# Dense adjacency matrices built by one-hot matmuls: float32 against bf16, with weights and sigmoids in three bf16 parts

## The chip, the cores and the metric

The kernel runs on one core of one Trainium2 chip. The metric is the device time of one execution in microseconds, shorter being better.

## The reference

A chain of four graph layers over 6250 nodes of 128 features and 200,000 edges (`src`, `dst`, sorted by `dst`), each ahead of which the features are normalised:

```python
h = relu(layernorm(x)); x = x + L0(h)   # edge score * sigmoid(sum(edge_attr_16)), segment mean
h = relu(layernorm(x)); x = x + L1(h)   # agg = segment_sum(x[src], dst)
h = relu(layernorm(x)); x = x + L2(h)   # two layers: agg = segment_sum(x[src] * w[:, None], dst)
h = relu(layernorm(x)); x = x + L3(h)   # attention over the edges, softmax by dst
```

L0, L1 and L2 need, for each pair of nodes, the number of edges between them, the sum of their edge weights and the sum of their sigmoids, so three dense matrices.

## The kernel before

The first stage builds the three matrices. Edges are cut into tiles of 128 and destinations into pairs of neighbouring nodes; a *step* is one tile of edges against one pair of destinations, and there are BSTEPS = 4704 of them. For a step, `place_hot` (128 edges x 128 places, one-hot by the low part of the source number, field F_LO) is TensorE's stationary operand, and `prod` (128 edges x 300 columns) the moving one. Its 300 columns are three segments of SEG = 100: COUNTED is a one-hot of 98 columns by block and parity (F_Q), WEIGHTED and SIGMOID are the same one-hot times the edge's weight (F_W) and sigmoid (F_SIG), and the last two columns of a segment hold F_DST. The sums accumulate in four banks of PSUM (`banks`), one per pair, in turn.

Four engines take part, tied by semaphores:

- VectorE makes `place_hot` and `prod` for BATCH = 8 steps at once (`make_steps`), in two buffers each; batch i waits until the steps of batch i - 2 are done (`step_added`).
- TensorE (`add_steps`) has per step a matmul of two zero columns that opens the next bank (line 1035, waiting on `pair_copied` for the copy of step j - 2) and the main matmul (line 1040). At every fourth step it first loads two sets of four bank numbers into registers (lines 1027 and 1030).
- ScalarE (`copy_pairs`) copies 3 x 100 columns of the previous pair's bank into `evac` at every step (line 888), behind the main matmul of step j - 1 and its own last copy; at every fourth step it loads two sets of four registers (lines 875 and 878).
- SP stores a round of 16 steps (`evac`, three transfers of 800 KB) to the matrices `adj` in memory (line 554); a round's store waits for the one ahead of it, and `evac` has two halves.

Every 128 steps (a *chunk*) a new table of the steps' fields is needed: an indirect DMA brings the rows `step_stage`, VectorE shifts them (`shift_rows`), TensorE transposes the five fields into PSUM (`turn_step_rows`, line 1015), and ScalarE copies them to `step_tab` (`take_tab`, lines 863 and 864). The loops over two chunks are unrolled. The stages behind this one read `adj` and don't change.

## Time and profile before

| | |
|---|---|
| median of 3 runs | 8950.64 us (8950.48 to 8950.79) |
| the profiled execution | 8941.34 us, span 8939.4 us |
| matrices are built | 146 to 4131 us of the span |
| TensorE, share of the span busy | 79% |
| VectorE, ScalarE, GpSimd | 42%, 30%, 20% |
| mean granted clock | 0.916 of 2.4 GHz |

A row names a line of the kernel, an engine (PE TensorE, PEld its weight loads, PEldq its sequencer, DVE VectorE, ACT ScalarE), what is written and read, and its size. Times of matmuls are modelled and overlap: the distance from start to start says more than a duration. A float32 matmul stands as two rows. In brackets stands how long the engine was idle ahead of a row, and what released it. "issue" is idle time for which no releaser is seen.

### The profile page before, as it was taken

To read this page: it belongs to the slowest core of one execution; us is meant where nothing else is said; L and a number is where in the kernel's file an instruction comes from. 1 tells how busy PE (TensorE), PEld (TensorE's weight loads), DVE (VectorE), ACT (ScalarE), POOL (GpSimd) and SP (SyncE) were. 2 spreads that over 40 slices of the span, in tenths; PEclk is the share of its full clock that TensorE was granted. 3 is DMA by queue.
4 is the path that set the end of the run, shared out by engine and by line. 5 is a ranking of instruction groups with operands and counts; after the bars stand their busy time and mean duration, and the time that the engine had idled before them with its cause. 6 is when DMAs were issued, how large, how long until landed. Compare 5 with 4: busy or idle time off the path is not lost.

```text
span 8939.4 us, 161519 instructions
## 1 busy us (share of the span) xinstructions
PE 7083.8 (79%) x43583; PEld 5299.3 (59%) x43583; DVE 3710.8 (42%) x6066; ACT 2678.1 (30%) x7276; POOL 1800.6 (20%) x1742
## 2 busy tenths in 40 slices
PE   3888888888888888888999999999954566565656
PEld 1444444444444444446999999999953444443444
DVE  5555555555555555554222111111122334333333
ACT  2444444444444444443111110000021122221222
POOL 1000000000000000000000000000037777777772
PEclk9999999999999999999999999999976777777777
DMA  6444444444444444446666666776622222222221
GB/s 190 189 182 187 185 185 186 185 187 183 189 180 186 185 187 186 180 187 250 258 258 270 276 277 277 279 279 278 276 60 54 57 57 55 57 54 57 56 57 35
DMA packets 261018, 1545.71 MB, mean 173 GB/s; under 512 B 56005, under 2 KB 88469, under 8 KB 233680
## 3 DMA queue, kind: packets, MB, share of 16 engines
q1 hardware_dynamic: 201528, 1406.81, 40.3%
q0 software_dynamic: 58704, 129.89, 6.0%
q8 instruction: 346, 5.67, 0.3%
q14 instruction: 310, 2.54, 0.1%
q10 hardware_dynamic: 130, 0.80, 0.0%
HBM read 795.79 MB, written 743.11 MB: 172 GB/s over the span
## 4 chain that ended last, share of the span: by engine, by line
PE 61%; issue 11%; ACT 10%; POOL 6%; ACTq 6%; DVE 4%; DMA 2%; SPq 0%; DVEq 0%; POOLq 0%
PE psum L1074 25%; PE psum L1040 23%; ACT field L888 8%; POOL field L778 5%; PE psum L1263 4%; PE psum L1241 4%; ACTq L878 2%; PE psum L1035 2%; ACTq L875 1%; ACTq L888 1%; ACT field L979 1%; DVE work L1767 1%; DMA field<-head_table,cmp 1%; DVE work L1771 1%; PE psum L1261 1%
## 5 line engine op out<-in xcount | busy, mean ns | idle before, releaser
L1040 PE MATMUL psum<-field 128*128 128x300 f32 x9408 | 3165.8, 468 | 30.2 <-DVE field L1475 4.7
L888 ACT COPY field<-psum x4704 | 1921.6, 408 | 2050.1 <-PE psum L1040 1040.8
L1074 PE MATMUL psum<-field 128*128 128x128 f32 x19208 | 2254.8, 277 | 23.6 <-issue 18.5
L1074 PEld LDWEIGHTS psum<-field 128*128 128x128 f32 x19208 | 2231.9, 189 | 24.0 <-issue 24.0
L1040 PEld LDWEIGHTS psum<-field 128*128 128x128 f32 x9408 | 1446.4, 194 | 612.2 <-issue 519.7
L778 POOL DMA_INDIRECT field<-head_table,cmp x1563 | 1630.5, 1043 | 476.3 <-issue 456.5
L1035 PEld LDWEIGHTS psum<-zero_b 128*128 128x128 bf16 x4704 | 462.9, 98 | 1442.9 <-issue 1246.8
L1035 PE MATMUL psum<-zero_b 128*128 128x2 bf16 x4704 | 801.4, 170 | 628.0 <-issue 405.2
L1470 DVE TENSOR_TENSOR field<-iota,field 128x784 f32<-128x784 f32 x588 | 574.0, 976 | 1636.9 <-PE psum L1040 1634.5
L1475 DVE TENSOR_TENSOR field<-field 128x784 f32<-128x784 f32 x1176 | 1090.9, 970 | 0.0
L722 POOL DMA_INDIRECT field<-tile_rows,step_t_i x37 | 40.3, 1090 | 3663.1 <-PE psum L1015 3619.2
L979 ACT COPY field<-psum x1611 | 432.0, 268 | 1022.5 <-PE psum L1263 701.4
L1263 PE MATMUL psum<-field,params 128*128 x3222 | 734.4, 348 | 1.2 <-issue 0.2
L1471 DVE TENSOR_TENSOR field<-iota,field 128x1024 f32<-128x1024 f32 x588 | 716.5, 1219 | 0.0
L1263 PEld LDWEIGHTS psum<-field,params 128*128 128x128 f32 x3222 | 538.1, 209 | 61.7 <-issue 1.8
L1819 DVE TENSOR_TENSOR params<-iota,cmp 128x1024 f32<-128x1024 f32 x202 | 247.2, 1224 | 662.7 <-PE psum L1263 662.7
L1241 PE MATMUL psum<-field,cmp 128*1 128x132 f32 x3126 | 477.6, 317 | 51.4 <-DVE field L1816 51.4
L928 ACT COPY work<-psum 128x128 f32<-128x128 f32 x196 | 52.3, 267 | 1546.5 <-PE psum L1114 1546.5
L732 POOL DMA_DIRECT2D tab_d<-field x3 | 4.6, 1518 | 2346.4 <-DVEq L1675 2333.3
L1261 PE MATMUL psum<-zero_b 128*128 128x2 bf16 x1611 | 283.4, 176 | 170.7 <-ACT field L979 169.0
L1241 PEld LDWEIGHTS psum<-field,cmp 128*1 128x1 f32 x3126 | 280.6, 95 | 215.0 <-DVE field L1816 56.0
L1207 PE MATMUL psum<-ident,field 128*64 128x128 f32 (+1 forms) x100 | 25.5, 408 | 449.5 <-DMA field<-head_table,cmp 449.5
(276 smaller groups left out, 2599.0 us busy)
## 6 DMA issues: line engine op xcount, KB each, us to landing
adj<-field SPq DMA_DIRECT2D x882, 800.0 KB, 4.9
field<-adj SPq DMA_DIRECT2D x196, 3200.0 KB, 10.0
field<-head_table,cmp POOLq DMA_INDIRECT x1563
field<-in_edge_attr SPq DMA_DIRECT2D x4, 3072.0 KB, 25.0
head_table<-field SPq DMA_DIRECT2D x7, 476.0 KB, 3.3
right_edges<-zeros SPq DMA_DIRECT2D x1, 3328.0 KB, 19.8
place_rows<-right_edges SPq DMA_DIRECT2D x25, 128.0 KB, 2.8
out<-X SPq DMA_DIRECT2D x6, 448.0 KB
```

Source lines behind the costliest of these rows:

```text
L778: pool.indirect_dma_start(out=rows3[:, (i * WIN + t) * ROW3:(i * WIN + t + 1) * ROW3], out_offset=None, in_=head_table, in_offset=bass.Ind ...
L888: act.copy(evac[half][:, :, bass.ds(place[j % 4], SEG)], banks[:, bass.ds(bank[j % 4], NSEG * SEG)].rearrange("p (w c) -> p w c", w=NSEG)) ...
L979: act.copy(AGGX[:, bass.ds(at[j % 4], AGG_W)], banks[:, bass.ds(bank[j % 4], AGG_W)]).then_inc(block_copied, 1)
L1035: pe.matmul(banks[:, bass.ds(after[j % 4], 2)], zero_b[:, :], zero_b[:, 0:2], start=True, stop=True, skip_group_check=True)
L1040: pe.matmul(banks[:, bass.ds(cur[j % 4], NSEG * SEG)], place_hot[buf][:, j % BATCH, :], prod[buf][:, j % BATCH, :], start=False, stop=True ...
L1074: mm = pe.matmul(ps_y[slot][:, 0:D], source[:, hi, :], adj_in[slot][:, :, 2 * hi:2 * hi + 2], start=(hi == 0), stop=(hi == NB - 1))
L1241: mm = pe.matmul(ps_seam[0:1, 0:AGG_W], win_tab[:, i, T_CARRY, e:e + 1], rows[:, i * WIN + e, :, 0:DH3 + 1], start=(e == 0), stop=(e == ti ...
L1261: pe.matmul(banks[:, bass.ds(after[j % 4], 2)], zero_b[:, :], zero_b[:, 0:2], start=True, stop=True, skip_group_check=True)
L1263: pe.matmul(banks[:, bass.ds(cur[j % 4], AGG_W)], hot3[:, t // SUB % HOTS, j % SUB, :], rows3[:, bass.ds(row[j % 4], ROW3)].rearrange("p ( ...
L1470: dve.tensor_tensor(first, counting(HI2), per_step(F_Q, HI2), ALU.is_equal).then_inc(group_hot, 1)
L1471: dve.tensor_tensor(hot, counting(P), per_step(F_LO, P), ALU.is_equal)
L1475: ins = dve.tensor_tensor(pr[:, :, seg * SEG:seg * SEG + HI2], first, per_step(field, HI2), ALU.mult)
```

## The change

The one-hots are made in bf16, where 0 and 1 are exact. A weight or sigmoid is split into three bf16 parts (the value rounded, the rest rounded, the rest of the rest), each times the one-hot gives a segment of its own, and TensorE adds them up in PSUM: `prod` has 1 + 2 x 3 = 7 segments, and the one matmul of 300 columns becomes one of 300 (counts and first parts) and two of 200 (second and third parts) into the same bank, with the same stationary operand. In `prod` and `place_hot` the eight steps of a batch are innermost: a step's columns lie 8 elements of 2 bytes apart. The small comparison against `iota` becomes one against `iota_b`, a bf16 table in the same order, made once. `split_parts` makes the parts, once per chunk.

```diff
--- before.py
+++ after.py
@@ -42,7 +42,10 @@
 BANKS = 4
 SLOTS = PAIRS + 2 * ROUND
 FIELDS = 5
-F_LO, F_Q, F_W, F_SIG, F_DST = range(FIELDS)
+F_LO, F_Q, F_DST, F_W, F_SIG = range(FIELDS)
+PLAIN = 3
+PARTS = 3
+TAB_FIELDS = PLAIN + 2 * PARTS
 COUNTED, WEIGHTED, SIGMOID = range(NSEG)
 KINDS = 4
 R_CUR, R_NEXT, R_PREV, R_PLACE = range(KINDS)
@@ -210,10 +213,12 @@
 
         piece = carve(arena)
         evac = [piece(NSEG * ROUND * SEG).rearrange("p (w c) -> p w c", w=NSEG) for _ in range(2)]
-        prod = [piece(BATCH * NSEG * SEG).rearrange("p (s c) -> p s c", s=BATCH) for _ in range(2)]
-        place_hot = [piece(BATCH * P).rearrange("p (s c) -> p s c", s=BATCH) for _ in range(2)]
+        prod = [piece(BATCH * (1 + 2 * PARTS) * SEG // 2).bitcast(BF16).rearrange("p (c s) -> p c s", s=BATCH) for _ in range(2)]
+        place_hot = [piece(BATCH * P // 2).bitcast(BF16).rearrange("p (c s) -> p c s", s=BATCH) for _ in range(2)]
         step_stage = [piece(FIELDS * P).rearrange("p (k e) -> p k e", k=FIELDS) for _ in range(2)]
-        step_tab = [piece(FIELDS * P).rearrange("p (k s) -> p k s", k=FIELDS) for _ in range(2)]
+        step_tab = [piece(TAB_FIELDS * P // 2).bitcast(BF16).rearrange("p (k s) -> p k s", k=TAB_FIELDS) for _ in range(2)]
+        iota_b = piece(P * BATCH // 2).bitcast(BF16).rearrange("p (c s) -> p c s", s=BATCH)
+        step_rest = piece(2 * P).rearrange("p (k s) -> p k s", k=2)
 
         piece = carve(arena)
         adj_in = [piece(BPAIRS * SEG).rearrange("p (g c) -> p g c", c=SEG) for _ in range(CRING)]
@@ -258,7 +263,7 @@
         psum = ctx.enter_context(nc.psum_tensor("psum", [P, 8 * BANK], F32))
         ps = [psum[:, i * 2 * BANK:(i + 1) * 2 * BANK] for i in range(4)]
         banks = psum[:, 0:BANKS * BANK]
-        ps_tab = [psum[:, 4 * BANK:5 * BANK], psum[:, 5 * BANK:5 * BANK + P]]
+        ps_tab = [psum[:, 4 * BANK:4 * BANK + PLAIN * P], psum[:, 5 * BANK:5 * BANK + 2 * P]]
         ps_y = [psum[:, i * BANK:i * BANK + 2 * D] for i in range(CRING)]
         ps_t = psum[:, 3 * BANK:3 * BANK + D]
         ps_kv = psum[:, 4 * BANK:4 * BANK + 2 * D]
...
@@ -860,8 +867,8 @@
             def take_tab(c, slot):
 
                 act.wait_ge(step_rows_turned, c + 1)
-                act.copy(step_tab[slot][:, 0:4, :], ps_tab[0].rearrange("p (k s) -> p k s", k=4))
-                act.copy(step_tab[slot][:, 4, :], ps_tab[1]).then_inc(step_tab_ready, 1)
+                act.copy(step_tab[slot][:, PLAIN:PLAIN + 2, :], ps_tab[1].rearrange("p (k s) -> p k s", k=2))
+                act.copy(step_tab[slot][:, 0:PLAIN, :], ps_tab[0].rearrange("p (k s) -> p k s", k=PLAIN)).then_inc(step_tab_ready, 1)
 
             def copy_pairs(k, n):
 
@@ -1011,8 +1018,10 @@
                 pe.wait_ge(step_rows_shifted, c + 1)
                 if not (isinstance(c, int) and c == 0):
                     pe.wait_ge(step_tab_ready, c)
+                    pe.wait_ge(step_parts_taken, c)
                 for i in range(FIELDS):
-                    mm = pe.transpose(ps_tab[i // 4][:, i % 4 * P:(i % 4 + 1) * P], step_stage[slot][:, i, :], ident[:, :])
+                    at = i % PLAIN * P
+                    mm = pe.transpose(ps_tab[i // PLAIN][:, at:at + P], step_stage[slot][:, i, :], ident[:, :])
                 mm.then_inc(step_rows_turned, 1)
 
             def add_steps(k, n):
@@ -1037,8 +1046,14 @@
                     if j % BATCH == 0:
                         pe.wait_ge(batch_ready, k * (PER_LOOP * CHUNK // BATCH) + (j // BATCH + 1))
                     buf = j // BATCH % 2
-                    pe.matmul(banks[:, bass.ds(cur[j % 4], NSEG * SEG)], place_hot[buf][:, j % BATCH, :], prod[buf][:, j % BATCH, :],
-                              start=False, stop=True, skip_group_check=True).then_inc(step_added, 1)
+                    hot, pr = place_hot[buf][:, :, j % BATCH], prod[buf][:, :, j % BATCH]
+                    pe.matmul(banks[:, bass.ds(cur[j % 4], NSEG * SEG)], hot, pr[:, 0:NSEG * SEG],
+                              start=False, stop=True, skip_group_check=True)
+                    for part in range(1, PARTS):
+                        col0 = (1 + 2 * part) * SEG
+                        mm = pe.matmul(banks[:, SEG:][:, bass.ds(cur[j % 4], 2 * SEG)], hot, pr[:, col0:col0 + 2 * SEG],
+                                       start=False, stop=True, skip_group_check=True)
+                    mm.then_inc(step_added, 1)
                     if at == CHUNK // 2 and not isinstance(k, int):
                         turn_step_rows(k * PER_LOOP + slot + 1, (slot + 1) % 2)
 
@@ -1437,8 +1452,8 @@
             dve.wait_ge(tile_rows_stored, 32)
             for i in range(2):
                 c.then(dve.memset(evac[i], 0.0))
-                c.then(dve.memset(prod[i][:, :, HI2:SEG], 0.0))
-                c.then(dve.memset(prod[i][:, :, SEG + HI2:2 * SEG], 0.0))
+                c.then(dve.memset(prod[i], 0.0))
+            c.then(dve.tensor_copy(iota_b, iota[:, :].rearrange("p (c s) -> p c s", s=1).to_broadcast([P, P, BATCH])))
             dve.sem_inc(banks_cleared, 2)
 
             def shift_rows(c_, slot, u=0):
@@ -1449,6 +1464,20 @@
                     ins = dve.tensor_scalar(t, t, col(step_off[:, i, :], c_), None, ALU.add)
                 ins.then_inc(step_rows_shifted, 1)
 
+            def split_parts(chunk, slot):
+
+                tab = step_tab[slot]
+                whole = ps_tab[1].rearrange("p (k s) -> p k s", k=2)
+                dve.wait_ge(step_tab_ready, chunk + 1)
+                dve.tensor_tensor(step_rest, whole, tab[:, PLAIN:PLAIN + 2, :], ALU.subtract).then_inc(step_parts_taken, 1)
+                dve.wait_ge(step_parts_taken, chunk + 1)
+                dve.tensor_copy(tab[:, PLAIN + 2:PLAIN + 4, :], step_rest).then_inc(part_ready, 1)
+                dve.wait_ge(part_ready, chunk * 3 + 1)
+                dve.tensor_tensor(step_rest, step_rest, tab[:, PLAIN + 2:PLAIN + 4, :], ALU.subtract).then_inc(part_ready, 1)
+                dve.wait_ge(part_ready, chunk * 3 + 2)
+                dve.tensor_copy(tab[:, PLAIN + 4:PLAIN + 6, :], step_rest).then_inc(part_ready, 1)
+                dve.wait_ge(part_ready, chunk * 3 + 3)
+
             def make_steps(k, n):
 
 
@@ -1456,24 +1485,22 @@
                     slot, at = i * BATCH // CHUNK, i * BATCH % CHUNK
                     hot, pr, tab = place_hot[i % 2], prod[i % 2], step_tab[slot]
                     if at == 0:
-                        dve.wait_ge(step_tab_ready, k * PER_LOOP + (slot + 1))
+                        split_parts(k * PER_LOOP + slot, slot)
 
                     dve.wait_ge(step_added, k * (PER_LOOP * CHUNK) + (i * BATCH - BATCH + ADDED0))
 
                     def per_step(field, m):
-                        return tab[:, field, at:at + BATCH].rearrange("p (s a) -> p s a", a=1).to_broadcast([P, BATCH, m])
-
-                    def counting(m):
-                        return iota[:, 0:m].rearrange("p (a m) -> p a m", a=1).to_broadcast([P, BATCH, m])
-
-                    first = pr[:, :, 0:HI2]
-                    dve.tensor_tensor(first, counting(HI2), per_step(F_Q, HI2), ALU.is_equal).then_inc(group_hot, 1)
-                    dve.tensor_tensor(hot, counting(P), per_step(F_LO, P), ALU.is_equal)
-                    dve.tensor_tensor(pr[:, :, 2 * SEG + HI2:3 * SEG], counting(2), per_step(F_DST, 2), ALU.is_equal)
+                        return tab[:, field, at:at + BATCH].rearrange("p (a s) -> p a s", a=1).to_broadcast([P, m, BATCH])
+
+                    first = pr[:, 0:HI2, :]
+                    dve.tensor_tensor(first, iota_b[:, 0:HI2, :], per_step(F_Q, HI2), ALU.is_equal).then_inc(group_hot, 1)
+                    dve.tensor_tensor(hot, iota_b, per_step(F_LO, P), ALU.is_equal)
+                    dve.tensor_tensor(pr[:, SIGMOID * SEG + HI2:(SIGMOID + 1) * SEG, :], iota_b[:, 0:2, :], per_step(F_DST, 2), ALU.is_equal)
                     dve.wait_ge(group_hot, k * (PER_LOOP * CHUNK // BATCH) + (i + 1))
-                    for seg, field in ((WEIGHTED, F_W), (SIGMOID, F_SIG)):
-                        ins = dve.tensor_tensor(pr[:, :, seg * SEG:seg * SEG + HI2], first, per_step(field, HI2), ALU.mult)
-                    ins.then_inc(batch_ready, 1)
+                    parts = pr[:, SEG:, :].rearrange("p (k c) s -> p k c s", c=SEG)[:, :, 0:HI2, :]
+                    dve.tensor_tensor(parts, first.rearrange("p (a c) s -> p a c s", a=1).to_broadcast([P, 2 * PARTS, HI2, BATCH]),
+                                      tab[:, PLAIN:, at:at + BATCH].rearrange("p k (a s) -> p k a s", a=1)
+                                      .to_broadcast([P, 2 * PARTS, HI2, BATCH]), ALU.mult).then_inc(batch_ready, 1)
                     if at == CHUNK // 4 and not isinstance(k, int):
                         shift_rows(k * PER_LOOP + slot + 1, (slot + 1) % 2, k + slot)
```

Line numbers of the order rows below are each kernel's own. A register operation or a wait stands as ISA or REGISTER_ALU.

TensorE, before, one step inside a group of four (line 1035 zero matmul, 1040 main matmul):

```order
L1034 REGISTER_ALU
L1035 ISA
L1035 MATMUL psum<-zero_b 128x2
L1040 ISA
L1040 MATMUL psum<-field 128x300
```

and in the changed kernel (1044 the zero matmul, 1050 the matmul of 300 columns, 1054 those of the second and third parts):

```order
L1043 REGISTER_ALU
L1044 ISA
L1044 MATMUL psum<-zero_b 128x2
L1050 ISA
L1050 MATMUL psum<-field 128x300
L1054 ISA
L1054 MATMUL psum<-field 128x200 x2
```

One register operation and two matmuls came in behind the main one; what comes ahead of it stays.

VectorE, before, the wait and one batch of eight steps (1470 the one-hot of 98, 1471 `place_hot`, 1472 the F_DST columns, 1475 the two products):

```order
L1461 ISA
L1470 TENSOR_TENSOR field<-iota,field 128x8x98
L1471 TENSOR_TENSOR field<-iota,field 128x1024
L1472 TENSOR_TENSOR field<-iota,field 128x8x2
L1473 ISA
L1475 TENSOR_TENSOR field<-field 128x8x98 x2
```

and in the changed kernel, with the split at the start of a chunk ahead of the batch (1472 to 1479 `split_parts`, 1496 to 1498 the comparisons, 1501 the product):

```order
L1472 TENSOR_TENSOR field<-psum,field 128x256
L1474 CAST field<-field 128x256
L1475 ISA
L1476 TENSOR_TENSOR field<-field 128x256
L1477 REGISTER_ALU
L1478 CAST field<-field 128x256
L1479 REGISTER_ALU
L1490 ISA
L1496 TENSOR_TENSOR field<-field 128x784
L1497 TENSOR_TENSOR field<-field 128x1024
L1498 TENSOR_TENSOR field<-field 128x16
L1499 ISA
L1501 TENSOR_TENSOR field<-field 128x6x784
```

The two products of 784 elements became one of 6 x 784, and four operations of 256 elements came in once per chunk.

## Rows read from the trace of the kernel before

**Rows 1.** The page: the span.

```profile
span 8939.4 us, 161519 instructions
```

**Rows 2.** Busy us (x instructions), clock, DMA share, GB/s, adjacency stage.

```profile
146.25:4131.10 3984.85, 3331.55 (x14290) 1929.12 (x14288) 2348.82 (x3013) 1939.90 (x4775) 37.86 (x35) 0.98 0.46 185
```

**Rows 3.** Groups by line, 300 to 4000 us: busy us, mean ns, idle before.

```profile
L1040 PE MATMUL psum<-field 128*128 128x300 f32 x8704 | 2931.6, 468 | 24.2 <-issue 3.4
L888 ACT COPY field<-psum x4352 | 1777.8, 408 | 1904.5 <-PE psum L1040 965.1 <-issue 548.3 <-ACT field L888 389.2
L1475 DVE TENSOR_TENSOR field<-field 128x784 f32<-128x784 f32 x1088 | 1009.4, 970 | 0.0
L1471 DVE TENSOR_TENSOR field<-iota,field 128x1024 f32<-128x1024 f32 x544 | 662.9, 1219 | 0.0
L1470 DVE TENSOR_TENSOR field<-iota,field 128x784 f32<-128x784 f32 x544 | 531.1, 976 | 1528.4 <-PE psum L1040 1528.4
```

**Rows 4.** Timeline, a group with short register loads: start, us, what, [idle].

```profile
2192.88 0.41 ACT L888 COPY field<-psum  x1 [0.19 <-PE psum L1040]
2193.81 0.41 ACT L888 COPY field<-psum  x1 [0.52 <-PE psum L1040]
2194.13 0.17 PE L1035 MATMUL psum<-zero_b 128*128 128x2 bf16 x1
2194.43 0.41 ACT L888 COPY field<-psum  x1 [0.22 <-PE psum L1040]
2194.74 0.17 PE L1035 MATMUL psum<-zero_b 128*128 128x2 bf16 x1
```

**Rows 5.** Timeline, a group with long register loads.

```profile
2003.49 0.41 ACT L888 COPY field<-psum  x1 [0.19 <-ACT field L888]
2005.11 0.10 PEld L1035 LDWEIGHTS psum<-zero_b 128*128 128x128 bf16 x1 [1.81 <-issue]
2005.23 0.30 PEld L1040 LDWEIGHTS psum<-field 128*128 128x128 f32 x2
2005.68 0.41 ACT L888 COPY field<-psum  x1 [1.79 <-issue]
```

**Rows 6.** The four register loads, by line: duration ns min/median/max.

```profile
L1027 PEldq TENSOR_LOAD <-bank_rows x1176: 327/335/1360, 138.8 to 4127.9; - x196
L1030 PEldq TENSOR_LOAD <-bank_rows x1176: 325/329/996, 139.4 to 4128.3; - x196
L875 ACTq TENSOR_LOAD <-bank_rows x1176: 303/311/1017, 140.2 to 4128.4; - x196
L878 ACTq TENSOR_LOAD <-bank_rows x1176: 302/307/1159, 140.7 to 4128.7; - x196
```

**Rows 7.** TensorE in a row elsewhere: chain of waits, timeline, groups by line.

```profile
5000.62 11.27 PE psum L1074 x98
...
303.67 0.71 PE L1015 MATMUL psum<-ident,field 128*128 128x128 f32 x5
...
138.48 1.33 PE L1015 MATMUL psum<-ident,field 128*128 128x128 f32 x5 [80.16 <-DVE field L1449]
...
6773.23 1.04 PE L1207 MATMUL psum<-ident,field 128*64 128x128 f32 x4 [138.45 <-DMA field<-head_table,cmp]
...
L1015 PE MATMUL psum<-ident,field 128*128 128x128 f32 x185 | 26.9, 277 | 80.2 <-DVE field L1449 80.2
...
L1207 PE MATMUL psum<-ident,field 128*64 128x128 f32 x96 | 24.9, 414 | 449.5 <-DMA field<-head_table,cmp 449.5
```

**Rows 8.** Groups by line, VectorE's scans, 6700 to 8900 us.

```profile
L1767 DVE TENSOR_TENSOR_SCAN work<-params,work 64x512 f32<-64x512 f32 x48 | 59.7, 1243 | 1.6
...
L1747 DVE TENSOR_TENSOR_SCAN work<-field,right,place_rows 64x128 f32<-64x128 f32 x92 | 36.9, 457 | 3.3 <-DVE field L1744 1.2
...
L1784 DVE TENSOR_TENSOR_SCAN work<-work 4x64 f32<-4x64 f32 x24 | 6.7, 278 | 0.8
```

**Rows 9.** Timeline, VectorE before the stage.

```profile
128.04 4.06 DVE L1439 MEMSET field<- 128x4800 f32 x1 [7.70 <-issue]
```

More of the change, by code:

```diff
@@ L306, in build @@
         step_tab_ready = sem("step_tab_ready")
+        step_parts_taken = sem("step_parts_taken")
+        part_ready = sem("part_ready")
         banks_cleared = sem("banks_cleared")
```

## The prediction

> **What bounds the kernel now.** I read the page first, then one row of busy times for the stretch in which the adjacency matrices are built, then the groups by line, and then the timeline inside that stretch. The changed code works only in this stretch, from the first main matmul to the last: 3984.85 us of the 8939.4 us span, for 4704 steps [rows 1 to 3]. That is 0.847 us a step, or 3.39 us for the group of four steps whose bank numbers are loaded together (1176 groups). The rest of the span does not change.
>
> TensorE looks like the bound: 3331.55 us busy of 3984.85 [rows 2]. The timeline says something else. Inside a group, steps follow each other at 0.61 to 0.62 us on TensorE (zero matmul at 2194.13 and at 2194.74) and the copies that empty the banks at 0.62 on ScalarE (2193.81, 2194.43) [rows 4]. Where ScalarE alone sets the pace, the copy costs 0.41 and the wait for its own predecessor 0.19, together 0.60: the 0.19 stands in brackets behind copies [rows 5]. So both engines stand at 0.60 to 0.62. Between groups both load two sets of four registers. Short loads take 0.33 us each on TensorE's sequencer and 0.31 on ScalarE's, long ones up to 1.0 us or more [rows 6]. With short loads the copy before and the copy after them start 0.93 apart (2192.88, 2193.81) [rows 4], with long ones 2.19 (2003.49, 2005.68) [rows 5]. So a group costs ScalarE 3 x 0.60 + 0.93 = 2.73 us at best and 3 x 0.60 + 2.19 = 3.99 at worst. With the long kind for the share of time in which stores run, 0.46 [rows 2], the mean is 0.54 x 2.73 + 0.46 x 3.99 = 3.31, against 3.39 measured. **ScalarE's copies and the register loads nearly explain the stage without TensorE's arithmetic.** What a faster matmul can win is small.
>
> **The change, part by part.**
>
> *TensorE's array.* Removed: one float32 matmul of 300 columns, done as two passes (8704 rows for 4352 steps [rows 3]), which with its loads and the zero matmul makes the 0.62 us. Added: three bf16 matmuls of 300 + 200 + 200 = 700 columns, whose columns lie 16 bytes apart, and three loads of 128 weights, 16 bytes apart too. No row shows a lone 2-byte column at such a step, so I bound it. Below: five contiguous float32 transposes in 0.71 us, of which one lasts 0.27, give 0.11 us per 128 columns in float32, 0.86 ns each [rows 7]; two bytes instead of four would be 0.43 ns, or 0.30 us for 700. Above, from three rows. Matmuls over the adjacency blocks read pairs of 8 bytes 400 bytes apart: 98 of them in 11.27 us, 0.115 us for 64 pairs, 1.80 ns a pair [rows 7]. So a fresh place costs at most 1.80 ns there. VectorE's scan over 128 elements 16 bytes apart takes 457 ns, while 64 contiguous take 278 [rows 8]; with 2.15 ns an element (1243 ns for 512) the contiguous 128 would be 416, so here the element costs about 2.5 ns, 1.75 us for 700. The third row speaks for cheap reads: at 1.2 GHz (0.21 us a transpose where the five at 2.4 GHz take 0.11) four transposes whose 64 weights lie 544 bytes apart start their last matmul 1.04 - 0.41 = 0.63 after the first (one lasts 0.41), exactly 3 x 0.21; five with 128 contiguous weights 1.33 - 0.41 = 0.92, which is 4 x 0.21 and 0.07 more for the first load [rows 7]. So 64 scattered weights took at most half as long as 128 contiguous ones, whose load is some 0.1 us (0.08 of it sticks out of the present step): about 0.85 ns each, where 1.80 ns would have stuck out. I take 0.85: 700 columns 0.60, first weight load 0.08 (the present step has 0.62 - 2 x 0.25 - 0.03 for it), zero matmul 0.03: **0.70 to 0.72 us a step**, about 2.85 a group. At 0.43 ns it is 0.41.
>
> *TensorE's sequencer.* A register operation, a weight load and a matmul take it 0.12 us (weight loads at 2005.11 and 2005.23, nothing else to wait for [rows 5]). The present step has two such and an addition (some 0.09), 0.33. The change adds another such and one load and matmul without a register operation (some 0.08, both estimates from the 0.12): 0.53 us. All register loads wait behind this. With short loads a group is 4 x 0.53 + 2 x 0.33 + 0.12 between them = 2.90, with long ones 4 x 0.53 + 1.9 + 0.12 = 4.14. Today the same sum is 2.1 and 3.3, and that slack is what the copies hide. It is gone.
>
> *VectorE.* Removed per batch of eight steps: 976 + 1219 + 2 x 970 ns [rows 3], with a small one of 0.17. Added: the same two comparisons in bf16 and one product of 6 x 784 = 4704 elements. At today's 1.04 ns an element and 0.16 fixed (784 in 0.97) the product is 5.06 and the batch 7.4 us. At half the bytes and half the time the batch is 0.57 + 0.69 + 0.17 + 2.61 = 4.0, what it is today, against 6.8 us for eight steps. I take 4.0, hidden behind TensorE; if that cover goes, the rival below prices it. The Trainium skill, "VectorE: DVE Perf Modes", section "The perf-mode tier table", has two-operand operations at twice the rate in bf16 and at one for float32; the float32 half agrees with [rows 3], the other no run here shows. The four split operations per 128 steps are some 2 us in a row before the batch at a chunk's start. VectorE is 2.8 us ahead there, so about 0.
>
> *ScalarE.* Two copies out of PSUM per 128 steps as now. Nothing changes: 0.
>
> *Stores.* Each 16 steps send three blocks of 800 KB as now; nothing moves but their share of time.
>
> *Start.* The two clears of the product buffer become 2 x 2800 words instead of some small ones; 4800 words took 4.06 us [rows 9], so 2.4 each, and a conversion about 1: +6 us, all engines wait for it.
>
> *The sum.* With short loads three limits stand together, 2.73 (copies), 2.85 (array) and 2.90 (sequencer), where now there is one. Engines that wait on each other two steps apart lose something each time: I put the group at 3.0. With long loads 4.14 + 0.05 = 4.2. The stores keep their amount, 0.46 x 3.39 = 1.56 us a group, of the new 3.55, so 0.44: 0.56 x 3.0 + 0.44 x 4.2 = 3.53. Now: 3.39, of which 0.08 are loop ends and the like that stay, already above the 3.31. On the same footing (3.31 to 3.53, and the five transposes a chunk no longer hidden, below 0.02 a group) I take +0.19 x 1176 = +223 us. **8941.34 + 223 + 6 = 9170 us** for the profiled execution (its time is the span and 2 us); the median of the plain runs is 9 us above it, which I leave out. Its own range is 8990 to 9350.
>
> **The rivals.**
>
> *1. A lone column 16 bytes on is dear (27%).* At 1.80 ns: 1.26 for columns, 0.23 for the weight load, 0.03: 1.52 us a step, 4704 x 1.52 = 7150. The register loads then hide behind the array, loop ends add 0.1 ms: 8941 - 3985 + 7270 = 12,230 us. At 2.5 ns: 1.75 + 0.32 + 0.03 = 2.1 a step, 14,900 us. It decides from about 0.9 ns a column on. For it: the pairs cost 0.115 us where contiguous float32 columns cost 0.108, and VectorE's scan. Against: the strided weights. The Trainium skill, "SBUF — State Buffer", has under "Specifications (TRN2)" 16-byte lines that need two hits each for full bandwidth, and every column here would be a first and only hit; it gives no price.
>
> *2. Faster: the copies alone set the pace (18%).* If TensorE's sequencer issues the two added pairs in well under 0.1 us each and the array needs 0.41 us a step, only ScalarE's 3.31 a group is left, without the losses of today: up to 0.08 x 1176 = 94 us less; if long loads also grow rarer because VectorE and TensorE read less, 0.2 a group, 235 us. Time 8700 to 8900. For it: slack of 0.2 us a step on the array. Against: the sequencer's 0.53. It decides where a step's issue is below 0.48 us.
>
> *3. VectorE keeps one element a cycle (5%).* 7.4 us and 0.2 of waits per batch, 588 batches: 4470 us in place of 3985, 9430 us. It decides when a batch is over 7 us.
>
> **How the numbers follow.** The likeliest case has 45%, rival 1 27%, rival 2 18%, rival 3 5%, no change 5%. The time is 9170. The range is 8750 to 12,400: it leaves out the dearer half of rival 1 and the far end of rival 2. A measurement of this kernel tells 0.2% (18 us) from no change. Faster 0.19, same 0.06, slower 0.75.
>
> **What would show it.** In the new profile: the first main matmul of a step to the next step's at 0.70 in a group (right), 0.41 (free reads) or 1.5 and more (rival 1). Register loads of 0.33 and 0.9 as now. ScalarE's idle time released by TensorE, not by itself. The product of VectorE at 2.6 us (5.1 for rival 3). A granted clock of 0.9 or less in this stretch where it is 0.98 [rows 2], that is more time at 1.2 instead of 2.4 GHz, since the array idles more behind the sequencer; at 0.85 ns a column it costs little. I am wrong if a strided column costs anything but 0.4 to 0.9 ns, or if the sequencer's work overlaps what I put in a row.

## The result, and the profile after

The changed kernel takes 11,069.33 us (median of 4 runs, 11,064.25 to 11,077.3) against 8950.56 for the kernel before: 1.2369 times as long, 95% interval 1.2347 to 1.239. The page's span, to hold against [rows 1]:

```profile
span 11075.5 us, 175316 instructions
```

The stage's window (busy us of PE, PEld, DVE, ACT and POOL with their instructions, granted clock, DMA share, GB/s), to hold against [rows 2]:

```profile
154.60:6263.70 6109.10, 6045.24 (x18993) 2304.27 (x18992) 2277.81 (x2570) 1955.17 (x4775) 68.31 (x35) 1.00 0.30 121
```

The stage took 3984.85 us and takes 6109.10: 2124 of the span's 2136 us. TensorE is busy for 99% of it where it was for 84%. The groups by line, 300 to 6000 us, answer to [rows 3]:

```profile
L1054 PE MATMUL psum<-field 128*128 128x200 bf16 x8770 | 3918.5, 536 | 0.0
L1050 PE MATMUL psum<-field 128*128 128x300 bf16 x4384 | 3046.0, 695 | 0.9
L895 ACT COPY field<-psum x4384 | 1800.6, 411 | 3877.0 <-PE psum L1054 3444.4 <-issue 388.7 <-ACT field L895 42.6
L1501 DVE TENSOR_TENSOR field<-field 128x4704 bf16<-128x4704 bf16 x549 | 1427.8, 2601 | 0.0
...
L1497 DVE TENSOR_TENSOR field<-field 128x1024 bf16<-128x1024 bf16 x548 | 374.7, 684 | 0.0
L1496 DVE TENSOR_TENSOR field<-field 128x784 bf16<-128x784 bf16 x548 | 310.8, 567 | 3573.2 <-PE psum L1054 3573.2
```

VectorE now waits for TensorE alone, and ScalarE mostly (3444 of its 3877 us of idle time). A matmul's mean duration (0.695 us) is not what it costs, since matmuls overlap; the starts in the timeline are (start, us, what), to hold against [rows 4]:

```profile
2192.39 0.19 PE L1044 MATMUL psum<-zero_b 128*128 128x2 bf16 x1
2192.44 0.69 PE L1050 MATMUL psum<-field 128*128 128x300 bf16 x1
2192.95 0.89 PE L1054 MATMUL psum<-field 128*128 128x200 bf16 x2
2193.67 0.19 PE L1044 MATMUL psum<-zero_b 128*128 128x2 bf16 x1
```

A step is 1.28 us from zero matmul to zero matmul: 0.05, then 0.51 for 300 columns, then 0.72 for twice 200. Over all steps the medians of the distances between the trace's starts are 48 ns (zero matmul), 515 (300 columns), 360 and 354 (200 columns each). That is 1.72 to 1.80 ns a column. VectorE's work beside it makes no difference: the median step is 1.276 us both for the 1104 steps in which VectorE is busy throughout and for the 2385 in which it does nothing. There is no pause where register loads stand: the step that follows them is 1.276 us like the others. The loads themselves (duration ns min/median/max) are as in [rows 6]:

```profile
L1036 PEldq TENSOR_LOAD <-bank_rows x1176: 327/332/967, 146.3 to 6256.3; - x196
L1039 PEldq TENSOR_LOAD <-bank_rows x1176: 325/328/1159, 146.9 to 6256.7; - x196
```

4704 x 1.276 = 6002 us. Of the other 107, some 66 are pauses at loop ends and some 38 are the five transposes, which add 1.04 us to one step in each chunk.

### The profile page after: what moved, and what is told of

Read it like the earlier page. It is cut to its first block, busy times and chain, and to the rows that moved or that the text cites. A ratio compares the mean times of both kernels' runs of the same rounds, so it can differ in the third digit from the quotient of the medians.

```text
span 11075.5 us, 175316 instructions
## 1 busy us (share of the span) xinstructions
PE 9807.5 (89%) x48287; PEld 5681.2 (51%) x48287; DVE 3644.7 (33%) x5625; ACT 2694.8 (24%) x7276; POOL 1839.8 (17%) x1742
## 4 chain that ended last, share of the span: by engine, by line
PE 83%; POOL 6%; issue 4%; DVE 3%; DMA 1%; ACT 1%; ACTq 0%; SPq 0%; DVEq 0%; POOLq 0%
PE psum L1054 30%; PE psum L1050 24%; PE psum L1089 20%; POOL field L785 5%; PE psum L1256 3%; PE psum L1278 3%; ACT field L986 1%; DVE work L1794 0%; DVE work L1798 0%; DMA field<-head_table,cmp 0%; PE psum L1276 0%; PE psum L1024 0%; DMA field<-in_edge_attr 0%; POOL right_edges L764 0%; DMA field<-adj 0%
## 5 line engine op out<-in xcount | busy, mean ns | idle before, releaser
L1054 PE MATMUL psum<-field 128*128 128x200 bf16 x9408 | 4203.6, 536 | 0.0
L1050 PE MATMUL psum<-field 128*128 128x300 bf16 x4704 | 3268.3, 695 | 6.9 <-DVE field L1501 6.1
L1054 PEld LDWEIGHTS psum<-field 128*128 128x128 bf16 x9408 | 1445.8, 154 | 1656.8 <-issue 1656.8
L1089 PEld LDWEIGHTS psum<-field 128*128 128x128 f32 x19208 | 2233.5, 189 | 18.1 <-issue 18.1
L1496 DVE TENSOR_TENSOR field<-field 128x784 bf16<-128x784 bf16 x588 | 333.5, 567 | 3818.6 <-PE psum L1054 3818.4
L1501 DVE TENSOR_TENSOR field<-field 128x4704 bf16<-128x4704 bf16 x588 | 1529.2, 2601 | 0.0
L1050 PEld LDWEIGHTS psum<-field 128*128 128x128 bf16 x4704 | 684.2, 145 | 1067.8 <-issue 1064.1
L1044 PEld LDWEIGHTS psum<-zero_b 128*128 128x128 bf16 x4704 | 595.3, 127 | 1074.0 <-issue 1074.0
L729 POOL DMA_INDIRECT field<-tile_rows,step_t_i x37 | 70.1, 1895 | 5575.7 <-PE psum L1024 5530.8
L1044 PE MATMUL psum<-zero_b 128*128 128x2 bf16 x4704 | 876.2, 186 | 63.2 <-issue 63.2
L1276 PE MATMUL psum<-zero_b 128*128 128x2 bf16 x1611 | 283.0, 176 | 174.0 <-ACT field L986 171.8
L1497 DVE TENSOR_TENSOR field<-field 128x1024 bf16<-128x1024 bf16 x588 | 402.0, 684 | 0.0
```

Of the source, the lines that this page charges most:

```text
L1044: pe.matmul(banks[:, bass.ds(after[j % 4], 2)], zero_b[:, :], zero_b[:, 0:2], start=True, stop=True, skip_group_check=True)
L1050: pe.matmul(banks[:, bass.ds(cur[j % 4], NSEG * SEG)], hot, pr[:, 0:NSEG * SEG], start=False, stop=True, skip_group_check=True)
L1054: mm = pe.matmul(banks[:, SEG:][:, bass.ds(cur[j % 4], 2 * SEG)], hot, pr[:, col0:col0 + 2 * SEG], start=False, stop=True, skip_group_chec ...
L1089: mm = pe.matmul(ps_y[slot][:, 0:D], source[:, hi, :], adj_in[slot][:, :, 2 * hi:2 * hi + 2], start=(hi == 0), stop=(hi == NB - 1))
L1496: dve.tensor_tensor(first, iota_b[:, 0:HI2, :], per_step(F_Q, HI2), ALU.is_equal).then_inc(group_hot, 1)
L1497: dve.tensor_tensor(hot, iota_b, per_step(F_LO, P), ALU.is_equal)
```

## The experiments

### The spacing of the columns, and who pays for it

Three kernels keep the change's arithmetic, its matmuls and the number of its weight loads, and alter only how many steps lie innermost: 4 (8 bytes from column to column), 2 (4 bytes), 1 (2 bytes, side by side; the product is then six instructions). VectorE's product is cut into as many operations as there are groups of steps, or, for 1, into one per part and kind. The weights' spacing changes with the columns'; a fourth kernel, e2_weights_dense, tells the two apart. The edit, here for 2 (`...` stands for parts left out):

```
+INNER = 2
-prod = [... .rearrange("p (c s) -> p c s", s=BATCH) ...]
+prod = [... .rearrange("p (g c s) -> p g c s", g=BATCH // INNER, s=INNER) ...]
-hot, pr = place_hot[buf][:, :, j % BATCH], prod[buf][:, :, j % BATCH]
+at_g, at_s = j % BATCH // INNER, j % INNER
+hot, pr = place_hot[buf][:, at_g, :, at_s], prod[buf][:, at_g, :, at_s]
```

**s4_inner.** 

> The changed kernel with four steps innermost instead of eight: a step's columns and weights lie 8 bytes apart, so two of them share 16 bytes; VectorE's product is two operations of 2352 elements. 
Measured: 9011.85 us, 1.0063 of before (1.0046 to 1.008). Steps in a row come to 0.653 to 0.657 us, as theory 'line' said, and the total to 38 us below its range; rival 'instructions' is out. Two stretches of its timeline on TensorE:

```profile
2190.22 0.18 PE L1045 MATMUL psum<-zero_b 128*128 128x2 bf16 x1
2190.27 0.43 PE L1052 MATMUL psum<-field 128*128 128x300 bf16 x1
2190.52 0.54 PE L1056 MATMUL psum<-field 128*128 128x200 bf16 x2
2190.87 0.19 PE L1045 MATMUL psum<-zero_b 128*128 128x2 bf16 x1
...
2196.88 0.43 PE L1052 MATMUL psum<-field 128*128 128x300 bf16 x1
2197.13 0.54 PE L1056 MATMUL psum<-field 128*128 128x200 bf16 x2
2197.49 0.19 PE L1045 MATMUL psum<-zero_b 128*128 128x2 bf16 x1
```

The windows around them (the third number from the end is the granted clock: 0.50 is 1.2 GHz, 1.00 is 2.4):

```profile
2189.40:2191.00 1.60, 1.57 (x10) 1.11 (x11) 1.60 (x4) 0.82 (x2) 0.00 (x0) 0.50 0.00 0
2196.00:2198.00 2.00, 2.00 (x16) 1.44 (x15) 2.00 (x4) 0.84 (x3) 0.71 (x1) 1.00 0.87 355
```

300 columns take 0.25 us at either clock (the median is 249 ns over the 2950 steps at 1.2 GHz and also over the 1580 at 2.4), 0.83 ns each, half of what they take at 16 bytes. The 200 columns take 181 ns, again at either clock. So in this kernel the clock doesn't set the price of a column.

**s2_inner.** 

> Two steps innermost: columns 4 bytes apart, four in 16 bytes; VectorE's product in four operations of 1176 elements, 3.1 us a batch. Theory 'line': full rate, 0.42 ns a column, 0.13, 0.09 and 0.09 us, about 0.4 us of array a step; the pace is then set by TensorE's sequencer (0.53 us a step and its register loads) or by ScalarE's copies (0.60), total 8850 to 9100. If the forecast's sum for the sequencer is right it is within 1% of 8950; if copies alone bind, 8700 to 8850. Rival 'instructions': 1.28 a step, 11,050.

Measured: 8943.09 us, 0.9989 (0.9979 to 0.9998), inside the 8850 to 9100 of theory 'line'. Its timeline on TensorE:

```profile
2189.89 0.31 PE L1052 MATMUL psum<-field 128*128 128x300 bf16 x1
2190.03 0.34 PE L1056 MATMUL psum<-field 128*128 128x200 bf16 x2
2192.22 0.18 PE L1045 MATMUL psum<-zero_b 128*128 128x2 bf16 x1 [1.85 <-issue]
...
2192.97 0.41 PE L1052 MATMUL psum<-field 128*128 128x300 bf16 x1
2193.18 0.53 PE L1056 MATMUL psum<-field 128*128 128x200 bf16 x2
2193.51 0.21 PE L1045 MATMUL psum<-zero_b 128*128 128x2 bf16 x1
```

The windows of these two stretches and of the whole stage:

```profile
2189.00:2190.00 1.00, 0.69 (x5) 0.32 (x5) 1.00 (x2) 0.81 (x3) 0.00 (x0) 1.00 1.02 416
2192.90:2194.40 1.50, 1.50 (x13) 1.11 (x11) 0.00 (x0) 0.83 (x3) 0.00 (x0) 0.50 1.00 410
156.40:4131.00 3974.60, 2950.72 (x18995) 1947.57 (x18992) 2402.19 (x4331) 1945.05 (x4774) 45.46 (x35) 0.69 0.47 186
```

VectorE's product, from the groups by line:

```profile
L1512 DVE TENSOR_TENSOR field<-field 128x1176 bf16<-128x1176 bf16 x2184 | 1534.4, 767 | 0.0
```

Now 300 columns take 0.14 us at 2.4 GHz and 0.21 at 1.2. So at 2.4 GHz the array does a step in less than the old 0.617 us, and it idles, and the clock of the stage goes from 0.98 [rows 2] to 0.69: some three fifths of the steps run at 1.2 GHz, where a step is 0.61 us again.

The lower clock is not what takes the gain. ScalarE's copies cost 0.60 us a step whatever the array does (0.41 and the 0.19 that the prediction read in [rows 5]). f_s2_16 below, the kernel with the fewest register loads, shows it at full clock (granted 0.99 from 2186 to 2192 us); its copies start 0.60 apart and 3796 of its 4703 distances lie between 595 and 605 ns:

```profile
2188.27 0.41 ACT L896 COPY field<-psum  x1 [0.19 <-ACT field L896]
2188.87 0.41 ACT L896 COPY field<-psum  x1 [0.19 <-PE psum L1056]
2189.47 0.41 ACT L896 COPY field<-psum  x1 [0.19 <-ACT field L896]
```

In s2_inner, too, half of the copies start within 0.601 us of the one ahead, and what the distances have above 0.60 sums to 1.16 ms, against 1.17 in the kernel before. TensorE's register loads sum to 1.28 ms, against 1.29. So the copies and the pauses stayed, and they are the stage: 4703 x 0.60 + 1.16 = 3.98 ms. A row of steps at 1.2 GHz is 0.01 us a step longer than the copies allow; what the lower clock costs behind each pause, where a faster array could catch up, no run separates.

**s1_inner.** 

> Columns of a step side by side (step outermost), every instruction of TensorE as in the changed kernel; VectorE now reads one value again and again along the innermost direction, product in six operations of 784. Theory 'line': TensorE's matmuls 0.13, 0.09 and 0.09 us apart inside a burst, no faster than with two innermost; VectorE at one element a cycle needs 0.97 + 1.22 + 0.17 + 6 x 0.97 = 8.2 us a batch and binds, total 9700 to 9900; if it keeps two a cycle there, as with two innermost. Rival 'instructions': 1.28 a step, 11,050.

Measured: 9429.16 us, 1.0531 (1.051 to 1.0552): VectorE binds, as theory 'line' said, but the time is 270 us below its range. TensorE's intervals are those of s2_inner (135 ns for 300 columns at 2.4 GHz, 207 at 1.2). The loss is VectorE's. The window of the stage:

```profile
159.80:4617.00 4457.20, 3124.04 (x18995) 2132.99 (x18992) 4428.82 (x5505) 1943.21 (x4775) 1234.08 (x34) 0.60 0.41 166
```

The product, from the groups by line. With its factor repeated side by side it costs 1.07 ns an element again (0.993 us less some 0.15 fixed, for 784):

```profile
L1508 DVE TENSOR_TENSOR field<-field 128x784 bf16<-128x784 bf16 x2926 | 2642.7, 993 | 0.0
```

VectorE is busy for 4429 of 4457 us. A batch takes it 7.5 us (4429 over 588 batches) and not the 8.2 that was expected, since its operations overlap by some 0.09 us each: six products keep it busy for 5.4 us, not for 6 x 0.993. This is rival 3 of the prediction, in a kernel that meets its condition (a batch over 7 us).

**e2_weights_dense.** The changed kernel, whose weights are read side by side:

```
-hot, pr = place_hot[buf][:, :, j % BATCH], prod[buf][:, :, j % BATCH]
+hot = place_hot[buf].rearrange("p c s -> p (c s)")[:, j % BATCH * P:(j % BATCH + 1) * P]
+pr = prod[buf][:, :, j % BATCH]
```

> The changed kernel, but TensorE reads the 128 weights of a step side by side from the same buffer (other values, so the sums are not the reference's); the moving columns stay 16 bytes apart. Theory 'line' on the moving operand: the 0.045 us ahead of the first matmul may fall to 0.03, a step stays at 1.25 to 1.28, total 11,000 to 11,070. Rival 'weights' (four loads with scattered reads hold up the array): a step falls to 0.8 or less, total below 9500.

Measured: 11,015.59 us, 1.2303 (1.2278 to 1.2328), in the range of theory 'line'; rival 'weights' is out. Its timeline on TensorE shows 0.51, 0.71 and 0.05, nearly those of the changed kernel:

```profile
2190.01 0.69 PE L1051 MATMUL psum<-field 128*128 128x300 bf16 x1
2190.52 0.89 PE L1055 MATMUL psum<-field 128*128 128x200 bf16 x2
2191.23 0.19 PE L1044 MATMUL psum<-zero_b 128*128 128x2 bf16 x1
```

A step is 1.263 us in place of 1.276. The spacing of the weights, three loads of 128, is worth 13 ns of a step; that of the columns 0.62 us from 16 to 8 bytes alone.

### Register loads, once the array is fast

The prediction had put the register loads between groups beside the copies as what bounds the kernel before. Four kernels read 8 or 16 numbers at a time:

```
-if j % 4 == 0:
+if j % 8 == 0:
-    ... bank_rows[0:1, slot, R_CUR, at:at + 4] ...
+    ... bank_rows[0:1, slot, R_CUR, at:at + 8] ...
```

**f_before8** (the kernel before). 

> The kernel before, with eight bank numbers per register load in place of four, so the two loads on TensorE and on ScalarE come every eighth step. Theory 'copies and loads set the pace': half of what a group costs above four copies goes, about 0.4 us of the 3.28 per four steps, 1176 x 0.4 = 470 us, total 8450 to 8550. Rival 'TensorE's float32 matmul sets the pace' (3332 of 3985 us busy): at most the 0.1 to 0.2 us in which the array really idles, total above 8800.

**f_s2_8** (s2_inner). 

> Two steps innermost and eight bank numbers per load. Theory 'copies and loads': as the kernel before with eight, and a little better since the array (0.34 us a step at 2.4 GHz, 0.61 at 1.2) no longer stands beside the copies (0.60): 8350 to 8500. Rival 'the array at 1.2 GHz binds' (it idles more, so its clock falls): no better than the kernel before with eight, 8450 to 8600.

**f_s2_16** (s2_inner, 16 numbers). 

> Two steps innermost and sixteen bank numbers per load. A round of sixteen steps is then 16 x 0.60 + 0.4 to 1.6 us, about 10.6 in place of 13.1: total 8150 to 8350; it stops falling if the stores bind (three of 800 KB take 7 to 8.5 us and each round's wait for the last's), then 8350 or more. Rival 'array at 1.2 GHz': 16 x 0.61 and no gain over eight numbers beyond 50 us.

**f_after8** (the changed kernel). 

> The changed kernel (eight innermost) with eight bank numbers per load. Theory 'its array binds at 1.28 us a step and hides the loads': 11,040 to 11,075, no change. If the loads still cost something behind the array, some 200 us less.

| | expected, us | measured, us | of before |
|---|---|---|---|
| f_before8 | 8450 to 8550; rival above 8800 | 9192.03 | 1.0271 (1.0253 to 1.029) |
| f_s2_8 | 8350 to 8500; rival 8450 to 8600 | 8851.08 | 0.9891 (0.9873 to 0.9909) |
| f_s2_16 | 8150 to 8350, or more | **8813.15**, the fastest kernel of all | 0.9845 (0.9828 to 0.9863) |
| f_after8 | 11,040 to 11,075 | 11,087.28 | 1.2387 (1.236 to 1.2414) |

Theory 'copies and loads' had the price of the loads wrong: what a group costs above its copies isn't halved, and on the kernel before the edit loses. f_before8 is above 8800, but not for the reason that its rival gave, since none of that rival's terms makes it slower. f_after8 is within 18 us of the changed kernel, whose array hides the loads. TensorE's loads in f_before8 (ns min/median/max):

```profile
L1027 PEldq TENSOR_LOAD <-bank_rows x588: 587/690/2433, 137.4 to 4363.6; - x196
L1030 PEldq TENSOR_LOAD <-bank_rows x588: 585/590/1999, 138.3 to 4365.4; - x196
```

A short load of 4 numbers takes 327 ns, one of 8 takes 587, one of 16 some 1100: 65 ns a number and 67 fixed. The long ones grow in the same way, from 0.93 us to 1.83, and they are long while stores run: of the 1176 first loads of the kernel before (line 1027) 585 run while a store's transfers are in flight, and 97% of these are long; of the other 591 one is. Fewer loads save only the fixed part: TensorE's loads sum to 1.11 ms in f_before8, 1.29 before. Why the kernel before even loses shows in f_before8's timeline on TensorE:

```profile
2005.88 0.75 PE L1040 MATMUL psum<-field 128*128 128x300 f32 x2
2008.43 0.17 PE L1035 MATMUL psum<-zero_b 128*128 128x2 bf16 x1 [1.80 <-issue]
2008.64 1.36 PE L1040 MATMUL psum<-field 128*128 128x300 f32 x2
2009.80 0.21 PE L1035 MATMUL psum<-zero_b 128*128 128x2 bf16 x1
```

The windows ahead of the pause and behind it:

```profile
2004.00:2005.80 1.80, 1.80 (x10) 1.20 (x9) 0.83 (x1) 1.18 (x4) 0.00 (x0) 1.00 1.04 427
2008.70:2011.00 2.30, 2.30 (x5) 1.29 (x6) 2.30 (x6) 0.68 (x2) 0.00 (x0) 0.50 0.03 8
```

Counted from the start of a step's second pass to the next zero matmul, this pause is 2.21 us; in groups with a long load it is 2.57 on average (1.49 in the kernel before). The steps behind this one run at 1.2 GHz, where a float32 step takes 1.2 us instead of 0.62. It isn't so behind each pause (the next, with 1.86 us of idle time, is followed by steps at 2.4 GHz: granted clock 1.00 from 2023.1 to 2026 us), but behind 32% of those with a long load, against 5% in the kernel before. Counted over the stage, 543 first passes take over 0.5 us (0.64 in place of 0.336) against 124 before; with the second pass of each that is 326 us lost in place of 75. The difference, 251 us, is about the 237 us that f_before8 is slower. It is an account and not an experiment, since no run holds the clock. A bf16 step at 4 bytes loses little at 1.2 GHz, which fits the small gain that f_s2_8 keeps.

**Loads apart.** The second load of each group is moved half a group on, on both engines (TensorE's edit is shown):

```
 if j % 4 == 0:
     _, cur = ... bank_rows[0:1, slot, R_CUR, at:at + 4] ...
-    _, after = ... bank_rows[0:1, slot, R_NEXT, at:at + 4] ...
+if at == 0 or at % 4 == 2:
+    end = min(2 if at == 0 else at + 4, CHUNK)
+    after0 = j
+    _, after = ... bank_rows[0:1, slot, R_NEXT, at:end] ...
```

**g_before_apart.** 

> The kernel before, with the two register loads of each group of 4 steps two steps apart instead of back to back (on TensorE: the bank numbers of the steps at step 0 of a group, those of the banks to clear at step 2; the same for the copies' two loads on ScalarE). Nothing else changes; one more load in each 128 steps. In the kernel before, the largest pause of TensorE in a group of 4 is 432 ns on average where its two loads are short (659 ns together), and 1488 ns where at least one is long (1567 ns together). Theory 'pause': the instructions that stand ready in TensorE's queue cover about 230 ns of each pause, once; apart, they cover it twice, so a group gains about 230 ns: 1176 x 0.23 = 0.27 ms, about 8680 us. Rival 'sum': what the loads cost is their sum, wherever they stand: 8930 to 8970 us.

**g_before8_apart.** 

> The kernel before with 8 numbers per register load, and the two loads of a group of 8 steps four steps apart. With 8 per load back to back the kernel took 9192 us; its largest pause in a group with a long load was 2.57 us on average, and the rest of such a group took 5.87 us against 5.04 us in a group with short loads, for the same 8 steps, at a granted clock of 0.92 instead of 0.97 in the stage. Theory 'pause and clock': apart, a pause is one load (0.59 us short, 1.8 us long) less 230 ns, the clock falls less often, and the kernel comes back to 8550 to 8750 us. Rival 'sum': about 9190 us, and the clock stays at 0.92.

**g_s2_apart.** 

> The form with two steps innermost (8943 us), with the two register loads of a group of 4 steps two steps apart. Theory 'pause': as in the kernel before, about 230 ns a group: 8650 to 8750 us. Here the clock is mostly at its lower level and the queue issues four weight loads and four matmuls a step, so the queue itself needs 0.451 us a step and has less time to run ahead; rival 'queue': no gain, 8920 to 8960 us.

**g_s2_16_apart.** 

> The fastest form so far (two steps innermost, 16 numbers per load, 8813 us), with the two loads of a group of 16 steps eight steps apart. A load of 16 takes 1.10 us short and about 1.9 us long. Theory 'pause': each of the two loads is covered by 230 ns instead of both together: 294 groups x 0.23 = 0.07 ms, 8740 to 8790 us, and less of the clock's fall. Rival 'sum': 8800 to 8820 us.

In this batch the kernel before itself took 9670.95 us, so only ratios to it count; the expectations, in us, are divided by 8950 here:

| | expected | measured, of before |
|---|---|---|
| g_before_apart | 0.970; rival 0.998 to 1.002 | 1.1009 (1.0975 to 1.1042) |
| g_before8_apart | 0.955 to 0.978; rival 1.027 | 0.9921 (0.989 to 0.9952) |
| g_s2_apart | 0.966 to 0.978; rival 0.997 to 1.001 | 1.0885 (1.0849 to 1.0922) |
| g_s2_16_apart | 0.977 to 0.982; rival 0.983 to 0.985 | 0.9853 (0.9826 to 0.9881) |

The stage of g_before8_apart ended 69 us earlier than that of the kernel before in its own trace, and what follows took 5.5 ms in place of 4.8, so most of the batch's extra time lies behind the stage. With 8 numbers, apart is better than together (0.992 for 1.027), as "pause and clock" said, though less than it forecast. With 16, apart is worth nothing (0.985 for 0.985), as rival 'sum' said. With 4, apart is 9 to 10% slower in both kernels, which neither theory allows. TensorE's loads in g_before_apart (ns min/median/max):

```profile
L1030 PEldq TENSOR_LOAD <-bank_rows x1176: 325/331/1014, 139.3 to 5101.6; - x196
L1036 PEldq TENSOR_LOAD <-bank_rows x1213: 535/1007/3303, 139.8 to 5103.7; - x174
```

and the moved load in g_before8_apart:

```profile
L1036 PEldq TENSOR_LOAD <-bank_rows x625: 330/593/1857, 140.1 to 4058.8; - x157
```

The expectations took a moved load to cost what it cost in its old place. In g_before_apart it doesn't, and the traces show on what that depends, if only loads with no store in flight are counted. Four numbers that start at a multiple of four in their row take 329 ns (line 1030). Four that start two further on, as the edit has it, take 1005 (571 loads). The two numbers at either end of a chunk take 537. That is 235 ns a number and 67 fixed. In g_before8_apart the moved loads start at multiples of four again and keep their price: 591 ns for eight numbers, 332 for four. g_s2_apart has 1005 and 537 like g_before_apart. So it isn't being apart that makes a load dear; a load that consists of whole groups of four numbers (16 bytes) is cheap. Why that is so no run shows.

The window from 300 to 4000 us of f_before8:

```profile
300.00:4000.00 3700.00, 2993.71 (x12462) 1794.71 (x12461) 2045.03 (x2626) 1692.27 (x4165) 52.83 (x32) 0.92 0.44 174
```

The same window of g_before_apart:

```profile
300.00:4000.00 3700.00, 2863.71 (x10652) 1621.14 (x10652) 1748.80 (x2246) 1448.76 (x3558) 41.11 (x28) 0.86 0.37 149
```

The same window of g_before8_apart:

```profile
300.00:4000.00 3700.00, 3079.52 (x13482) 1816.54 (x13480) 2211.38 (x2839) 1830.53 (x4506) 40.63 (x33) 0.98 0.47 188
```

The stage of g_before_apart is 976 us longer than before. TensorE's loads sum to 2.29 ms in it in place of 1.29, ScalarE's to 2.28 in place of 1.17. The clock adds its part: it is 0.92 with one long pause a group, 0.98 with two shorter ones and 0.86 in g_before_apart, where slow passes cost 595 us against 75 before, which is half of the 976. In g_before8_apart they cost 67, against 326 in f_before8, and its stage is 313 us shorter than that kernel's.

## Why the prediction was wrong

**The direction was right and the place was right; the size was off by a factor of ten.** Forecast +219 us on the plain runs, measured +2119. That the measured time lies inside the stated range, 8750 to 12,400, is due to the room that the range left for rival 1.

*The step that failed* is the array's term, at "I take 0.85": the price of a column at 16 bytes. It was drawn from the row of strided weights, which is a row of the weights' read and not of the columns'. e2_weights_dense shows that weights hardly mind their spacing (13 ns a step), and s4_inner and s2_inner show that columns do: 1.72, 0.83 and 0.48 ns for 16, 8 and 4 bytes at 2.4 GHz. The upper bound that stood beside it, the pairs at 1.80 ns a fresh place [rows 7], hit the price to 5%. That is luck as far as the row goes: two float32 columns in 1.80 ns are 0.90 each, next to the 0.86 of contiguous ones, so the row only bounds what a fresh place costs and says nothing of a lone bf16 column. Forecast 0.70 to 0.72 us a step, measured 1.276: 0.566 x 4704 = 2.66 ms, less 0.76 ms of pauses that the forecast kept (4.21 ms of stage less 0.71 x 4704, against 0.11 measured) and that a busy array hides, makes the 1.90 ms by which the stage was missed.

*The sum* has a slip besides: 3.31 to 3.53 and below 0.02 for the transposes are 0.22 to 0.24 us a group, not 0.19. By its own terms the forecast would have been 36 to 59 us higher, still within its range.

*What bounds the kernel before* was read rightly, as far as it goes: with the array's matmuls faster and everything else kept, s2_inner gains 0.1%, and where most register loads are gone the copies start 0.60 us apart (f_s2_16). What the reading lacked is the clock: a long pause costs itself and, in a float32 kernel, the slow steps that at times follow it.

*Rival 1* (27%) is what happened. It said 1.52 us a step: 1.26 for the columns, right (0.515 + 0.360 + 0.354 = 1.23), and 0.23 for the weight load, wrong, since strided weights are cheap. Without that its sum would have been 11.1 ms. It also had the register loads hidden and the decision at 0.9 ns.

*The lines of 16 bytes.* The Trainium skill, "SBUF — State Buffer", section "Specifications (TRN2)", with its 16-byte lines that need two hits for full bandwidth, pointed the right way. By these runs it holds for the columns: the time halves from 16 to 8 bytes, and at 8 bytes it is the same at both clock levels. It doesn't hold in price for the weights, and two hits a line (8 bytes) are not yet TensorE's full rate at 2.4 GHz: that takes 4 bytes.

*TensorE's sequencer.* Forecast 0.53 us a step; the shortest distance of two steps on it is 0.451 in s2_inner, which has the same matmuls and loads (0.322 before, forecast 0.33), 65 ns for each added pair. It never mattered in the changed kernel.

*VectorE.* Right: 0.567 + 0.684 + 0.159 + 2.601 = 4.01 us a batch, forecast 4.0. Twice the rate in bf16 holds with 8, 4 or 2 steps innermost and ends at 1 (rival 3).

*The clock.* Forecast to fall to 0.9 or less; it rose to 1.00, with the array busy for 99% of the stage. The fall came in s2_inner (0.69), where the array is busy for 74%.

*The start.* Forecast +6 us, measured 9 (the first main matmul at 153.7 for 144.9). *Loads of registers* as in [rows 6], as said.

*Rival 2* (a fast array gives up to 235 us) can be judged by s2_inner. With columns at 4 bytes the array is fast and the sequencer's 0.451 is below the 0.48 that the rival asked for, and the copies do set the pace, yet the kernel gains 0.1%: the losses that the rival took away are still there. f_s2_16 comes to 8813, inside the rival's 8700 to 8900, but by fewer register loads, which the rival didn't have.

## What to carry to other kernels

Lay out what TensorE streams so that neighbouring bf16 columns lie at most 4 bytes apart, and let VectorE keep a short run (2 is enough) innermost for its bf16 rate: both are to be had together, and that is the 19% of the changed kernel's time that s2_inner saves. When a price isn't in the trace, ask of each row near it which operand's read it shows; weights and moving columns are two. A matmul that gets cheaper inside a chain of waits brings idle time and a lower clock, so look first for what else takes as long: here copies of 0.60 us a step, and pauses. Load registers in whole groups of four numbers that start at a multiple of four.

## What the runs showed of the hardware

- Moving columns in bf16 at 16 bytes cost 1.72 to 1.80 ns (300 in 515, 200 in 360), at 8 bytes 0.83 to 0.91 at both clock levels (300 in 249, 200 in 181), at 4 and 2 bytes 0.48 and 0.45 at 2.4 GHz (300 in 143 and 135).
- Weights at 16 bytes cost next to nothing more than weights side by side: 13 ns in a step with three such loads.
- A register load of whole groups of four numbers costs 65 ns a number and 67 ns fixed, and about three times that for 4 or 8 numbers while stores are in flight (0.93 and 1.83 us). Four numbers that start two past a multiple of four cost 1005 ns, two numbers 537.
- Behind a pause in which TensorE was idle for 1.80 us the granted clock was 0.50 for more than two steps, and a float32 step then took twice its time; behind another of 1.86 us it was not.
- VectorE multiplied two bf16 operands at 0.52 ns an element with rows of 8, 4 or 2 elements (1176 in 0.767 us, less 0.16), and at 1.07 where the factor's inner step is 0.
